# One transfer a unit for the sums of squared keys, and an earlier place for the end of feed-forward, in a fused two-layer block

## The chip, the cores and the metric

The kernel is one program on one core of a Trainium2 chip. The metric is the device time of one execution in microseconds, from the median of several runs. A core has TensorE for matrix products (PE in the profile; PEld is its weight load), VectorE (DVE), ScalarE (ACT), GpSimd (POOL) and SyncE (SP), which here only issues DMA transfers. Every engine works through its own list of instructions in order and waits on semaphores. 16 DMA engines carry the transfers of all of them.

## The reference

Batch 4, 512 positions, width 512, context 512 x 256, all in float32. Two layers stand one behind the other, each with a mixing step and a feed-forward step:

```
x = x + tanh(g_xattn[0]) * mamba(ctx, z=layernorm(x))        # 512 channels, 16 states, a scan over 512 positions
x = x + tanh(g_ffn[0])   * bit_ffn(layernorm(x))             # gate/val/out, 512 x 2048, ternary weights, 8-bit rows
x = x + tanh(g_xattn[1]) * attn(layernorm(x), ctx)           # 16 heads of 128, rmsnorm on q and k
x = x + tanh(g_ffn[1])   * experts(layernorm(x))             # 4 experts, row i goes to expert i % 4

# in attn:
k = (ctx @ Wk).reshape(B, S, 16, 128);  v = (ctx @ Wv).reshape(B, S, 16, 128)
k = k * rsqrt(mean(k ** 2, axis=-1) + 1e-5) * gk
```

The keys and values depend on the context alone. For each of 4 batches and 16 heads the kernel computes the keys, and for each key the mean of squares and its power -1/2.

## The kernel before

Six streams of work are written out as lists: Q (the ternary weights are made from the float weights), M (the scan, `MAMBA`, per batch b), F (the first feed-forward, `FFN`, per batch), K (keys and values, `KV`), A (attention, `ATTN`, 64 heads j = 16 b + head) and E (the experts). Each stream has a generator for every engine that yields once per item. `plan()` merges the streams: it gives each item the engines and times that are written in `mamba`, `forward`, `keys` and so on (microseconds, estimates in the source), their needs and PSUM banks, and always takes the item that can start first, ties by `FIRST`. What comes out is one fixed order of streams for each engine. At run time nothing is reordered: an instruction that waits holds up all that stand behind it on its engine.

**Keys and values, K.** A unit is (b, q): batch b and heads 4q to 4q+3; n = 4q + b runs from 0 to 15. In a unit TensorE forms four key blocks (`k`, L780) and four value blocks (`v`, L785), and ScalarE copies them to `ks` (three buffers; L1379, L1385) and squares the keys (L1382). Then `n` (L791) sums the squares by a product with ones, into four rows of a bank; `nv` (ScalarE, L1390) writes mean plus eps of these to `ksr`, of which there is one, after it has waited for the transfers out of `ksr` of the unit before. `r` (SP, L1742) issues four transfers from rows 0, 32, 64 and 96 of `ksr` to 32 partitions x 16 columns of `krs` each. `pw` (GpSimd, L1503) raises 128 x 16 values to -1/2, and `st` (SP, L1746) stores them to `rk_scratch`. `pw` and `st` of a unit stand in the next unit. Keys and values go to memory from SP, L1718 and L1724; the weights of the next group of heads are fetched at L1631 and L1636, in the places `v` 0 and `v` 3 of the last batch's unit. Attention's queries use the region of `ksr`.

**The scan, M.** For each of 32 steps VectorE runs a product (L1020), a scan (L1025) and a product (L1032) on 128 x 1024, ScalarE forms the decay (L1290), and GpSimd issues a transfer that adds the term to `u` (L1534), from one of three buffers. For b = 0 the factors come from TensorE (L666, L670).

**The first feed-forward, F.** For each group t of 128 rows: entry `e` 0 (statistics), 1 (quantization, VectorE), 2 (transposes), `o` (GpSimd adds a bias to x); then `m`, even numbers TensorE and ScalarE, odd ones VectorE, for four chunks of 512 of the hidden width; then leaving, `l` 0 (quantization of h, L1065 and L1069), `l` 1 and 2 (transposes L736, copies L1359), `l` 3 (the output product, L746) and `l` 4 (the addition to x, L1147). The leaving of group t stands between the items of group t+1. When all four groups are through, the list `XT` follows: `st` (statistics, L924, and deviation on GpSimd) for four t, `hn` (normalization, L1159) for four t, `xt` (transposes L758, copies L1368) for four t. `hn` writes over h. Attention of a batch (`q`, L806) needs all four `xt`.

M of batch 0, Q and K run first, F of batch 0 behind M, then attention of batch b beside M and F of batch b+1, at the end the experts.

## Time and profile before

| | us |
|---|---|
| median of 3 runs | 1853.01 (1847.89 to 1858.5) |
| the profiled execution, its time | 1852.26 |
| its span, first to last instruction | 1850.5 |
| TensorE busy | 1763.2 (95%) |
| VectorE busy | 1300.1 (70%) |
| ScalarE busy | 963.8 (52%) |
| GpSimd busy | 666.5 (36%) |
| mean granted clock of TensorE | 0.983 |

The profile comes from one execution. Its page gives the busy time of each engine and 40 slices of the span; the trace behind it answers for stretches, lines of the source, waits (an engine's idle time just before an instruction, and what ended it), DMA issues with their time to landing, and the chain of work that ended last. The granted clock is the share of full speed that TensorE had. A row of the timeline may merge neighbours of one kind, with their count behind an x.

### The profile page before, as it was taken

Reading aid. Unit: us, or ns where it says so; the run is one execution under the profiler, and the core shown is the slowest. Engines: PE = TensorE matmul, PEld = TensorE weight load, DVE = VectorE, ACT = ScalarE, POOL = GpSimd, SP = SyncE. Lnnn points to the kernel's source line nnn. Section 1 sums busy time; section 2 is a strip of 40 time slices with the busy share of each in tenths; the row PEclk is TensorE's granted clock in tenths of the full one; section 3 lists DMA queues with packets and bytes.
Section 4 is the critical chain, followed back from the end, with each engine's and each line's share of the span. In section 5 each row is a group of like instructions: output and inputs, shape, how many; then the busy total and the mean of one; then the engine's idle time right before and its main releaser. Section 6 shows DMA issues by size and latency. Waiting matters only on the chain.

```text
span 1850.5 us, 19507 instructions
## 1 busy us (share of the span) xinstructions
PE 1763.2 (95%) x6114; PEld 809.9 (44%) x6114; DVE 1300.1 (70%) x1899; ACT 963.8 (52%) x1920; POOL 666.5 (36%) x696
## 2 busy tenths in 40 slices
PE   8999899879999999999999999999999899999999
PEld 4333344334444444444444444444444344445543
DVE  4989686989998689899787998987652444422221
ACT  7988786446545546566455566555435334320100
POOL 2434322337463324557222564562223333310000
PEclk9999899979999999999999999999999999999999
DMA  7999833767851146897212589732112799837110
GB/s 262 242 289 286 244 109 116 203 164 187 199 142 57 51 100 162 208 240 200 66 30 74 156 188 251 199 95 69 35 57 91 218 282 293 236 119 273 40 51 28
DMA packets 159045, 292.11 MB, mean 158 GB/s; under 512 B 18424, under 2 KB 51704, under 8 KB 156000
## 3 DMA queue, kind: packets, MB, share of 16 engines
q1 hardware_dynamic: 141664, 227.95, 39.0%
q0 software_dynamic: 17280, 62.92, 17.5%
q8 instruction: 50, 0.82, 0.2%
q14 instruction: 51, 0.42, 0.1%
HBM read 169.51 MB, written 58.26 MB: 123 GB/s over the span
## 4 chain that ended last, share of the span: by engine, by line
PE 72%; DVE 13%; ACT 6%; issue 4%; DMA 3%; POOL 1%; SPq 1%; DVEq 0%; ACTq 0%; POOLq 0%
PE p L846 11%; PE p L806 10%; PE p L823 9%; PE p L857 8%; PE p L893 6%; PE p L697 5%; DVE s_M L1025 5%; PE p L780 4%; PE p L829 4%; PE p L908 3%; PE p L746 3%; PE p L785 3%; DVE s_M L1020 2%; DVE s_M L1032 1%; DVE s_U L1178 1%
## 5 line engine op out<-in xcount | busy, mean ns | idle before, releaser
L1025 DVE TENSOR_TENSOR_SCAN s_M<-s_M 128x1024 f32<-128x1024 f32 x128 | 296.4, 2315 | 9.9 <-ACT s_M L1290 7.6
L1178 DVE CUSTOM_DVE_ANT_0 s_U<-p,s_U 128x512 f32<-128x512 f32 x256 | 188.2, 745 | 161.0 <-PE p L823 159.7
L823 PE MATMUL p<-s_U 128*128 128x512 f32 x512 | 268.2, 612 | 4.6 <-DVE s_U L1178 3.0
L806 PE MATMUL p<-s_U 128*128 128x512 f32 x512 | 256.7, 610 | 3.4 <-ACT s_U L1418 2.7
L1534 POOL DMA_DIRECT2D s_u<-s_M x120 | 111.7, 931 | 383.7 <-DVE s_M L1032 355.6
L1579 POOL TENSOR_SCALAR s_U<-s_U 128x512 f32<-128x512 f32 x256 | 231.9, 926 | 6.3
L857 PE MATMUL p<-s_U 128*128 128x512 f32 x512 | 223.7, 593 | 0.0
L846 PE MATMUL p<-s_U 128*128 128x512 f32 x472 | 216.0, 599 | 2.5 <-ACT s_U L1431 2.4
L1431 ACT COPY s_U<-p 128x512 f32<-128x512 f32 x196 | 105.5, 594 | 176.3 <-PE p L829 175.0
L1290 ACT ACTIVATE s_M<-s_dl,s_small 128x511 f32<-128x511 f32 x256 | 170.3, 717 | 35.5 <-DVE s_M L1025 35.3
L1426 ACT ACTIVATE s_U<-s_U 128x512 f32<-128x512 f32 x256 | 181.6, 710 | 5.3
L1575 POOL TENSOR_TENSOR s_U<-s_U,s_mone 128x4 f32<-128x4 f32 x64 | 81.7, 1277 | 201.1 <-ACT s_U L1426 201.0
L857 PEld LDWEIGHTS p<-s_U 128*128 128x128 f32 x512 | 96.8, 190 | 119.0 <-issue 118.1
L806 PEld LDWEIGHTS p<-s_U 128*128 128x128 f32 x512 | 96.1, 197 | 106.3 <-issue 87.1
L846 PEld LDWEIGHTS p<-s_U 128*128 128x128 f32 x472 | 89.9, 192 | 113.8 <-issue 108.0
L780 PE MATMUL p<-s_U 128*128 128x512 f32 x256 | 120.2, 615 | 18.9 <-ACT s_U L1390 10.8
L1503 POOL TENSOR_TENSOR s_U<-s_U,s_mhalf 128x4 f32<-128x4 f32 x64 | 80.7, 1261 | 136.7 <-ACT s_U L1418 136.0
L823 PEld LDWEIGHTS p<-s_U 128*128 128x128 f32 x512 | 88.2, 193 | 83.1 <-issue 77.8
L697 PE MATMUL p<-s_wq,s_U 128*128 128x512 fp8e4 x512 | 121.6, 380 | 0.0
L785 PE MATMUL p<-s_U 128*128 128x512 f32 x256 | 119.6, 601 | 2.1 <-ACT s_U L1382 1.5
L1032 DVE TENSOR_TENSOR s_M<-s_M,s_bc 128x1024 f32<-128x1024 f32 x96 | 119.8, 1248 | 1.4
L1020 DVE TENSOR_TENSOR s_M<-s_du,s_bc 128x1024 f32<-128x1024 f32 x96 | 116.8, 1216 | 0.0
(194 smaller groups left out, 2458.3 us busy)
## 6 DMA issues: line engine op xcount, KB each, us to landing
s_u<-s_M POOLq DMA_DIRECT2D x120, 512.0 KB, 7.6
s_bc<-bc_scratch SPq DMA_DIRECT2D x96, 256.0 KB, 4.5
k_scratch<-s_U SPq DMA_DIRECT2D x16, 1024.0 KB, 7.9
v_scratch<-s_U SPq DMA_DIRECT2D x16, 1024.0 KB, 5.4
s_U<-in_Wq SPq DMA_DIRECT2D x64, 256.0 KB, 6.6
s_U<-k_scratch SPq DMA_DIRECT2D x64, 256.0 KB, 5.4
s_U<-rk_scratch SPq DMA_DIRECT2D x64, 256.0 KB, 5.8
s_U<-in_Wo SPq DMA_DIRECT2D x64, 256.0 KB, 4.5
```

Of the source, the lines that this page charges most:

```text
L697: ins = e.matmul(banks[bk][:], xT[t % 2][:, k, :], wt[:, k, ch * 512:(ch + 1) * 512], start=False, stop=(k == 3))
L780: ins = e.matmul(banks[bk][:], wk[:, k, i * 128:(i + 1) * 128], cT[b][:, k, :], start=(k == 0), stop=(k == 1))
L785: ins = e.matmul(banks[bk][:], cT[b][:, k, i * 128:(i + 1) * 128], wv[:, k, :], start=(k == 0), stop=(k == 1))
L806: ins = e.matmul(banks[bk][:], wqq[j % 2][:, k, :], axT[b % 2][:, k, :], start=(k == 0), stop=(k == 3))
L823: e.matmul(banks[bk][:], qT[j % 3][:, k * 128:(k + 1) * 128], kT[j % 2], start=True, stop=True).then_inc(S["a_s"], 1)
L846: ins = e.matmul(banks[bk][:], V[v][:, kt, :], now[:, kt], start=(kt == 0), stop=(kt == 3))
L857: ins = e.matmul(banks[bk][:], OT[h][:, k * 128:(k + 1) * 128], wo[h], start=(i == 0), stop=(i == GH - 1))
L1025: e.tensor_tensor_scan(w, dA[i % 2], w, 0.0, ALU.mult, ALU.add).then_inc(S["m_s"], 1)
L1178: e.tensor_tensor_reduce(out=Pm[j % 2][:, k, :], in0=banks[ABANK[kind, j, k]][:], in1=rkb[j % 2], scale=rq[:, k:k + 1], scalar=-3.0e38, op ...
L1290: e.activation(av[:, t, 1:512], dl[:, 2 * g + t, 1:512], ACT.Exp, scale=Aneg[:, 2 * g + t, n:n + 1]).then_inc(S["m_da"], 1)
L1426: e.activation(Pm[j % 2][:, k, :], Pm[j % 2][:, k, :], ACT.Exp, bias=nm[:, k:k + 1], scale=1.0, accum_out=sm[:, k:k + 1]).then_inc(S["a_e" ...
L1579: e.tensor_scalar(P, P, rc[:, k - 1:k], 1.0, ALU.mult, ALU.mult).then_inc(S["a_pd"], 1)
```

## The change

- `ksr` becomes two buffers, used in turn; `nv` waits for the transfer two units before (unit 1 for the first product that read the region).
- `r` becomes one transfer, from the four rows of `ksr` to a new array `rs_scratch` in memory, 2 KB a row. It stands before `v` 3.
- A new item `ld` loads the 16 rows of four units, as 128 partitions x 64 columns of `krs`; it waits for the four transfers. `pw` comes four times, on 16 columns each, and `st` once, 128 x 64, both per four units. They stand in the units of the next group of heads: `ld` behind `k` 1 of its first unit, `pw` behind `k` 3, `st` in the second unit.
- `rk_scratch` has another order of rows; the loads of its rows in attention follow. Attention's first rows wait for the first store only, and before heads 4, 8 and 12 SP waits for the store of their group.
- The store of the keys and the fetch of the next `wk` move to the place of `k` 3.
- In `ffn_order` both transposes `l` 1 and 2 of the group before stand behind `m` 2, `l` 3 behind `m` 4, `l` 4 behind `m` 5; the next entry's statistics come before `m` 3, its `o` and transposes behind `m` 6.
- `XT` goes. `st` of groups 0 to 2 stands behind `l` 0 of group 3, `hn` and `xt` of these behind `l` 3, and `st`, `hn`, `xt` of group 3 last. `st` waits for the addition of its own group.
- Two semaphores are merged into others (`d_dtw` into `d_ipw`, `f_pad` into `p_set`); the planner's times follow.

```diff
-            order += [("m", t, 2 * c)] + (leave[:1] if c == 0 else []) + [("m", t, 2 * c + 1)] + (leave[3:] if c == 2 else leave[c + 1:c + 2] if c < 2 else [])
-            if c:
-                order += enter[:1]
-                enter = enter[1:]
-        order += enter
+            order += [("m", t, 2 * c)] + (leave[:1], leave[1:3], leave[3:4], enter[2:])[c]
+            order += (enter[:1] if c == 1 else []) + [("m", t, 2 * c + 1)] + (leave[4:] + enter[1:2] if c == 2 else [])
         leave = [("l", t, k) for k in range(5)]
-    return order + leave
+    order += leave[:1] + [("st", t, 0) for t in range(3)] + leave[1:4] + [("hn", t, 0) for t in range(3)] + [("xt", t, 0) for t in range(3)]
+    return order + leave[4:] + [("st", 3, 0), ("hn", 3, 0), ("xt", 3, 0)]
...
-XT = [("st", t) for t in range(4)] + [("hn", t) for t in range(4)] + [("xt", t) for t in range(4)]
...
 for q in range(4):
     for b in range(NB):
-        last = ((b - 1) % NB, q - (b == 0))
-        KV += [(b, q, "k", i) for i in range(4)] + [(b, q, "v", 0), (b, q, "v", 1), (b, q, "n", 0), (b, q, "v", 2), (b, q, "nv", 0)]
-        KV += [(*last, "pw", 0)] if q or b else []
-        KV += [(b, q, "v", 3), (b, q, "r", 0)] + ([(*last, "st", 0)] if q or b else [])
-KV += [(NB - 1, 3, "pw", 0), (NB - 1, 3, "st", 0)]
+        first, second = q > 0 and b == 0, q > 0 and b == 1
+        KV += [(b, q, "k", 0), (b, q, "k", 1)] + ([(NB - 1, q - 1, "ld", 0)] if first else []) + [(b, q, "k", 2), (b, q, "k", 3)]
+        KV += [(NB - 1, q - 1, "pw", i) for i in range(4)] if first else []
+        KV += [(b, q, "v", 0), (b, q, "v", 1), (b, q, "n", 0)] + ([(NB - 1, q - 1, "st", 0)] if second else [])
+        KV += [(b, q, "v", 2), (b, q, "nv", 0), (b, q, "r", 0), (b, q, "v", 3)]
+KV += [(NB - 1, 3, "ld", 0)] + [(NB - 1, 3, "pw", i) for i in range(4)] + [(NB - 1, 3, "st", 0)]
...
-        ksr = U[:, 26624:27136]
+        ksr = [U[:, o:o + 512] for o in (26624, 25600)]
...
-                        if n:
-                            e.wait_ge(S["d_ksr"], 64 * n)
-                        e.activation(ksr, banks[bk][:], ACT.Copy, bias=EPS, scale=1.0 / HD).then_inc(S["k_nv"], 1)
+                        if n == 1:
+                            e.wait_ge(S["m_xp"], 1)
+                        elif n:
+                            e.wait_ge(S[f"d_ksr{n % 2}"], 16 * (n // 2))
+                        e.activation(ksr[n % 2], banks[bk][:], ACT.Copy, bias=EPS, scale=1.0 / HD).then_inc(S["k_nv"], 1)
...
-                        n = NB * q + b
-                        power(krs[:, 16 * n:16 * n + 16], (S["d_ksr"], 64 * (n + 1)), "k_p")
+                        power(krs[:, 64 * q + 16 * i:64 * q + 16 * i + 16], (S["d_kr"], 16 * (q + 1)), "k_p")
...
-                    if kind == "v" and i == 0:
+                    if kind == "k" and i == 3:
                         if b == NB - 1 and q < 3:
                             load_kw(q + 1)
-                    elif kind == "v" and i == 1:
                         e.wait_ge(S["k_kc"], 4 * n + 4)
...
                         e.wait_ge(S["k_nv"], n + 1)
-                        for h in range(4):
-                            e.dma_start(krs[32 * h:32 * h + 32, 16 * n:16 * n + 16],
-                                        ksr[32 * h:32 * h + 1, :].rearrange("o (p c) -> o p c", c=16)).then_inc(S["d_ksr"], 16)
+                        e.dma_start(rsd[16 * q + 4 * b:16 * q + 4 * b + 4], ksr[n % 2][0:128:32, :]).then_inc(S[f"d_ksr{n % 2}"], 16)
+                    elif kind == "ld":
+                        e.wait_ge(S["d_ksr0"], 32 * (q + 1))
+                        e.wait_ge(S["d_ksr1"], 32 * (q + 1))
+                        e.dma_start(krs[:, 64 * q:64 * q + 64], rsd[16 * q:16 * q + 16].rearrange("r (p c) -> (r p) c", c=64)).then_inc(S["d_kr"], 16)
                     elif kind == "st":
-                        e.wait_ge(S["k_p"], n + 1)
-                        e.dma_start(rkd[j:j + 4].rearrange("h (p c) -> (h p) c", c=16), krs[:, 16 * n:16 * n + 16]).then_inc(S["d_rk"], 16)
+                        e.wait_ge(S["k_p"], 4 * (q + 1))
+                        e.dma_start(rkd[16 * q:16 * q + 16].rearrange("r (p c) -> (r p) c", c=64), krs[:, 64 * q:64 * q + 64]).then_inc(S["d_rk"], 16)
```

## Rows read from the trace of the kernel before

**Rows 1.** The page: busy time of TensorE; DMA share in 40 slices, tenths.

```profile
PE 1763.2 (95%) x6114; PEld 809.9 (44%) x6114; DVE 1300.1 (70%) x1899; ACT 963.8 (52%) x1920; POOL 666.5 (36%) x696
...
DMA  7999833767851146897212589732112799837110
```

**Rows 2.** Windows of 20 us: length, then busy times, clock, DMA share, GB/s; sums.

```profile
360.00:380.00 20.00, 9.51 (x40) 4.40 (x38) 19.52 (x24) 7.11 (x12) 6.63 (x7) 0.83 0.92 231
...
sum 840.00, PE 785.04 PEld 351.45 DVE 712.25 ACT 541.88 POOL 338.69; mean PE 18.69 PEld 8.37 DVE 16.96 ACT 12.90 POOL 8.06
...
sum 1020.00, PE 978.15 PEld 458.48 DVE 587.83 ACT 421.93 POOL 327.85; mean PE 19.18 PEld 8.99 DVE 11.53 ACT 8.27 POOL 6.43
```

**Rows 3.** Windows of 5 us around the large stall, same columns.

```profile
195.00:200.00 5.00, 0.00 (x0) 0.00 (x0) 0.00 (x0) 0.00 (x0) 0.00 (x0) 0.64 1.05 300
200.00:205.00 5.00, 4.10 (x5) 1.85 (x6) 3.18 (x4) 3.47 (x6) 3.03 (x2) 0.50 0.70 265
```

**Rows 4.** The chain that ended last: start, us, what.

```profile
186.89 13.29 DMA s_krs<-s_U
...
200.90 6.55 PE p L780 x8
207.89 3.43 PE p L780 x8
```

**Rows 5.** Timeline, 181 to 201 us: start, duration, instruction, idle before it.

```profile
181.40 0.36 SPq L1724 DMA_DIRECT2D v_scratch<-s_U  x1
...
200.24 2.90 POOL L1503 TENSOR_TENSOR s_krs<-s_krs,s_mhalf 128x16 f32<-128x16 f32 x1 [8.14 <-DMA s_krs<-s_U]
...
200.90 3.78 PE L780 MATMUL p<-s_U 128*128 128x512 f32 x4 [6.63 <-ACT s_U L1390]
```

**Rows 6.** DMA issues of 180 to 202 us: median us to landing last.

```profile
v_scratch<-s_U SPq DMA_DIRECT2D x1, 1024.0 KB, 18.1
```

**Rows 7.** Timelines of TensorE and of SP around the fetches of keys’ weights.

```profile
77.00 3.60 PE L780 MATMUL p<-s_U 128*128 128x512 f32 x8
...
94.45 6.02 PE L780 MATMUL p<-s_U 128*128 128x512 f32 x10 [5.36 <-DMA s_U<-in_Wk]
...
162.88 3.67 PE L780 MATMUL p<-s_U 128*128 128x512 f32 x8 [2.49 <-DMA s_U<-in_Wk]
...
82.59 1.14 SPq L1631 DMA_DIRECT2D s_U<-in_Wk  x1
```

**Rows 8.** Timeline of VectorE, around 105 us.

```profile
105.35 1.22 DVE L1020 TENSOR_TENSOR s_M<-s_du,p 128x1024 f32<-128x1024 f32 x1 [5.57 <-PE p L666]
```

**Rows 9.** The tile krs: its instructions, min/median/max ns.

```profile
L1742 SPq DMA_DIRECT2D s_krs<-s_U x64: 513/1036/1937, 41.8 to 366.6; - x64
L1503 POOL TENSOR_TENSOR s_krs<-s_krs,s_mhalf x16: 2903/4174/5304, 54.1 to 368.7; 128x16 f32<-128x16 f32 x16
```

**Rows 10.** Timeline, 376 to 386 us.

```profile
376.93 0.72 DVE L1147 SCALAR_TENSOR_TENSOR s_x<-p,s_fq,s_x 128x512 f32<-128x512 f32 x1
377.69 0.69 DVE L924 BATCH_NORM_STATS2 s_U<-s_x 128x6 f32<-128x512 f32 x1
...
380.81 0.64 POOL L1512 TENSOR_TENSOR s_U<-s_U,s_mhalf 128x1 f32<-128x1 f32 x1
...
381.57 3.65 PE L758 MATMUL p<-s_identf,s_U 128*128 128x128 f32 x16 [5.52 <-DVE s_U L1159]
...
385.93 6.19 PE L806 MATMUL p<-s_U 128*128 128x512 f32 x8 [0.72 <-issue]
```

**Rows 11.** Timeline of GpSimd, 85 to 91 us.

```profile
85.51 5.30 POOL L1503 TENSOR_TENSOR s_krs<-s_krs,s_mhalf 128x16 f32<-128x16 f32 x1
90.66 1.04 POOL L1534 DMA_DIRECT2D s_u<-s_M  x1
```

**Rows 12.** DMA issues, 60 to 200 us, and one of the whole run.

```profile
s_krs<-s_U SPq DMA_DIRECT2D x32, 2.0 KB, 7.3
...
bc_scratch<-s_M SPq DMA_DIRECT2D x3, 64.0 KB, 1.6
```

91 lines of the change are left out of this document (38 added, 53 removed).

## The prediction

> **What bounds the kernel now.** I read four views in this order: the page's busy times, the table of 20 us windows, the timeline of TensorE with its idle gaps, and for each large gap the chain and the waits of the other engines. TensorE is busy 1763.2 us of a span of 1850.5 us [rows 1]; the two halves of the window table give the same sum, 785.04 up to 840 us and 978.15 behind [rows 2]. Only idle TensorE time, 87.3 us in all, and time at its lower clock can be won by a new order. Of the idle time 55 us (840 less 785.04) lie before 840 us. There the kernel has two weak places. Up to about 210 us the DMA engines are full [rows 1], and TensorE waits for things that land late. Near 370 us the keys and values are used up, attention can't start, and TensorE is busy 9.51 of 20 us [rows 2]. After 420 us attention fills nearly every gap, so I expect what is won before to be carried to the end, and nothing to be won there.
>
> **The one large stall, around 195 us.** In 195 to 200 us no engine has any busy time, while the DMA share is 1.05 [rows 3]. ScalarE's `nv` (L1390) of unit 9 wants to overwrite the only `ksr`, whose four transfers of unit 8 are still on their way: the last was issued at 186.89 and landed 13.29 us later [rows 4]. GpSimd, which waits for the same transfers, ran at 200.24, and TensorE at 200.90 after 6.63 us idle, behind ScalarE's L1390 [rows 5]. The clock had fallen to 0.50 in 200 to 205 us [rows 3], the 1.2 GHz level, after 5 us without any matmul; eight matmuls took 6.55 us where the next eight took 3.43 [rows 4], so 3.1 us more were lost. Together 9.7 us. The change has two `ksr`, and `nv` waits for the transfer of two units before, so this wait goes. What is late next is a buffer of three, `ks`: the values of unit 8 were issued at 181.40 [rows 5] and took 18.1 us [rows 6], so they landed at 199.5, and the first key copy of unit 10 goes into their buffer. TensorE finished unit 9 at about 194.3 (200.90 less 6.63). It has three banks for k0 to k2, three times 1.72 us (half of 3.43 us), so it works to 199.5; k3 waits for ScalarE's two passes after 199.5, some 1.2 us. I take 9.7 less 1.2 = **8.5 us saved**, with ends 3 and 9.7: the low end holds if the DMA backlog itself makes all three wait until 199.5 or later (6.63 us idle less the 5.2 us from 194.3 to 199.5 leaves 1.4 us, and about half of the 3.1 us of clock, 3 in all).
>
> **The weights of the second group of heads.** TensorE waited 5.36 us, to 94.45, for `in_Wk` [rows 7], and VectorE in turn 5.57 us for a broadcast that stood behind those products [rows 8]. The weights may be fetched when the 16th key product is done, at 80.6 (77.00 plus 3.60), but the queue of SP was then in four `krs` transfers, a store and another load, and issued at 82.59 [rows 7]. The change replaces four issues of 1.036 us (median, up to 1.937) by one [rows 9], drops 12 of 16 stores, and puts the fetch two places earlier. That gives 82.59 less 80.7 = **1.9 us**. Ends: 0, since the 11.7 us of landing are the DMA engines' and not SP's, and 5.4 if the load also overtakes the 1 MB load ahead of it. The third group's fetch had 2.49 us of idle too, but was issued as the product ended; I give it nothing. Over 16 units the change takes 48 issues and 12 stores off SP, some 50 us times one microsecond; nearly all is hidden, as SP mostly waits for engines.
>
> **The end of the first feed-forward.** Before, the statistics of all four row groups wait for the last one. VectorE's last addition to x is at 376.93 (0.72 us, to 377.65), and the first product of attention starts at 385.93 [rows 10]: 8.3 us. Here run four statistics, GpSimd's two small steps, four normalizations, 16 transposes and a copy. After, three groups are through while the output product of the last group runs, and one remains. Three statistics of 0.8 us (the first at 377.69, 0.69 us and the aggregation behind it) leave the path, 2.4 us, and three quarters of the 3.65 us of transposes, 2.7 us. GpSimd's steps on the one group, hidden behind the next group's statistics before, now stand in the open: 0.64 us for the power and, as an estimate, as much again for the small step and the handovers, 1.3 us [rows 10]. 2.4 + 2.7 less 1.3 = **3.8 us saved**. VectorE does three statistics and three normalizations, some 4 us, in front of the last addition instead of behind it; they stand where it ran steps of the next scan while TensorE formed the output product, so they push those and not the addition. Without this cover they would cost their 4 us, and the saving would be 0. Ends 0 and 6: the latter if the shorter gap also spares the lower clock some two of the microseconds that it took from what follows 380 us, as it took 3.1 us behind the other gap.
>
> **The reordered middle of feed-forward.** TensorE now forms the second chunk's products before the first transposes, and both transposes stand together; VectorE's entry statistics come one product earlier. Per row group the same instructions run. Three of the four feed-forwards run beside attention, where other products are at hand: behind 840 us all causes together leave some 32 us idle (87.3 less 55) in a thousand. I take 0, with ends minus 2 and plus 3 us, a tenth of that. The joined semaphore of the first two weights costs nothing: they are issued one behind the other, and TensorE waits for the first at most once, while it still warms up.
>
> **What is added.** The squared sums go out to memory, come back as 64 columns for four units together, are raised to the power in four pieces, and go out again. The power work is the same, 16 pieces of 4.17 us median [rows 9], none of it on the end's path; but four stand in a row now, three times. GpSimd also issues the accumulating transfers of the scan (L1534), about every 5 us. A piece of 5.30 us beside a busy VectorE (2.90 when all was idle, [rows 5]) just fits between two of them: from 85.51, with the next issue at 90.66 [rows 11]. Four in a row are late by some 0.6 to 1 us each, 2.4 to 4 us per group, of which the landing slack takes a part. And there are two new waits in order: SP waits before the load for the last unit's store, and GpSimd before the first piece for the load. Behind SP's wait stand the next key store and weight loads; behind GpSimd's stand the accumulating transfers, and behind these VectorE's scan, which needs their buffers. The cover is two products on either side and the values between, about 8 us. An 8 KB transfer in the full stretch lands in 7.3 us (median of 32) and on a quiet queue a store of 64 KB in 1.6 us [rows 12]. At 7.3 us for each, store, load and issues take some 16 us against 8 to 12 us of cover; that is paid at most at the two group ends in the full stretch, less what the scan's three buffers absorb. I take **plus 3 us** for all of this, nearest to the single pieces that were absorbed; ends 0 and 12.
>
> The Trainium skill ("DMA: Bandwidth & Descriptors", the anatomy of one DMA) puts a fixed 2.0 us on each transfer, most of it the write receipt of the target memory. By that figure the store and the load would be an estimated 4 us, under the cover, and the sum would end 3 us lower, at 1838. The trace agrees for the quiet queue (1.6 us) and not for the full one (7.3 us), so the rows decide.
>
> **The sum.** 8.5 + 1.9 + 3.8 less 3 = 11.2 us. The profiled execution took 1852.26 us, 1.76 us more than its span, and lies 0.75 us below the median of the three runs, inside their spread. 1852.26 less 11.2 is **1841 us**.
>
> **The rivals.**
> (1) *The DMA engines bound the first 200 us.* For it: the share stays at about 1 from 60 to 200 us [rows 1], and the age of the backlog was 18.1 us [rows 6]. Then one wait gives way to the next: 3 us from the large stall, 0 from the weights, 3.8 from the tail, and 1 us of new waits remain against: 5.8 us, 1846.5. Against it: the share fell to 0.70 right behind the stall [rows 3], so the backlog ended there.
> (2) *GpSimd's order becomes the bound, the kernel is slower.* At the group ends near 97 and 168 us the store and the load each land as late as the slowest seen, 13.3 us [rows 4]; with issues 28.6 us against 10 us of cover. Each end then stops GpSimd, the scan and, through ScalarE's decays, TensorE for 18 us; twice 18 less 14.2 gives plus 22, 1874. It decides from 12 us per end (two of them beyond 14.2 plus 9.3). Against it: no such transfer but that one took so long, and scan and products have their own slack.
> (3) *More is won than counted.* The stall goes entirely, the weights overtake the load, the tail spares the clock, no new wait: 9.7 + 5.4 + 6 = 21, 1831.
> (4) *The large stall doesn't go*, since `nv` of unit 9 finds another wait of the same length (the `ks` buffer and the accumulating transfers land as late): 1.9 + 3.8 less 3, about 1849.5.
>
> **How the numbers follow.** Chances: forecast 0.43, (1) 0.20, (3) 0.18, (4) 0.12, (2) 0.07. About 0.5%, or 9.3 us, is what a measurement of this kernel can tell from no change: the bounds are 1843.7 and 1862.3. The forecast's own range, 1834 to 1849, lies two thirds to three quarters below 1843.7; with (3) and a little of (1) this gives 0.54 for faster. Slower is (2) with its larger half, 0.06; the rest, 0.40, is no change. The range from 1829 to 1852 leaves out (2) and the edges.
>
> **What would show it.** The 195 to 200 us window has busy engines and TensorE no gap above 2 us for L1390; SP issues `in_Wk` within 0.3 us of the 16th key product; from the last addition to x to the first product of attention it is about 4.5 us; GpSimd shows waits for the loaded squares of 0 to 6 us near 97 and 168 us, and four powers in a row; behind 420 us TensorE's idle time stays within 3 us of before. The prediction is wrong if the powers or their wait stop VectorE's scan for more than 6 us in all, or if the ScalarE wait at 193 us returns under another name.

## The result, and the profile after

The changed kernel takes 1859.43 us (median of 20 runs, 1851.65 to 1862.68), the kernel before 1851.78 us in the same comparison (20 runs, 1845.78 to 1858.5): a ratio of 1.0037, interval 1.0025 to 1.0049. The forecast was 1841 us with a range of 1829 to 1852, so the time moved the other way and lies outside the range. The profiled execution of the changed kernel took 1859.95 us, its span is 1858.2 us.

The page of the changed kernel: busy time, TensorE's clock and the DMA share, as in [rows 1].

```profile
PE 1767.5 (95%) x6114; PEld 808.6 (44%) x6114; DVE 1303.7 (70%) x1899; ACT 965.5 (52%) x1919; POOL 676.3 (36%) x696
...
PEclk9999999989999999999999999999999999999999
DMA  7999833688761138878113579822122799847110
```

TensorE is busy 4.3 us more for the same 6114 products, GpSimd 9.8 us more. The large stall is gone. Below are the same windows of 5 us as in [rows 3], and the last addition of feed-forward and attention's first product, as in [rows 10].

```profile
195.00:200.00 5.00, 5.00 (x13) 1.98 (x11) 3.38 (x2) 4.36 (x8) 4.83 (x4) 1.00 0.98 288
200.00:205.00 5.00, 5.00 (x18) 1.97 (x18) 3.63 (x6) 3.77 (x7) 4.83 (x5) 1.00 1.05 306
```

```profile
365.06 0.75 DVE L1139 SCALAR_TENSOR_TENSOR s_x<-p,s_fq,s_x 128x512 f32<-128x512 f32 x1 [1.65 <-PE p L742]
...
372.66 1.53 PE L798 MATMUL p<-s_U 128*128 128x512 f32 x3 [0.72 <-issue]
```

The first product of attention starts at 372.66 instead of 385.93, 13.3 us earlier. So the gains came, and were lost later. Behind 420 us TensorE is idle 45.4 us of 1430.5 before and 55.7 us of 1438.2 after (length, then TensorE's busy time, before and after):

```profile
420.00:1850.50 1430.50, 1385.14 (x4935) 650.09 (x4933) 958.97 (x1509) 664.06 (x1457) 524.54 (x580) 0.99 0.52 142
...
420.00:1858.20 1438.20, 1382.48 (x4895) 646.28 (x4894) 962.67 (x1508) 661.03 (x1443) 530.35 (x577) 0.99 0.52 141
```

The next table tells where, for this and all kernels below. Each row is one profiled execution, while executions of one kernel differ by some 10 us, so a difference of two or three us in one cell is not yet a property of the kernel. Its marks are starts of instructions in the timeline: q0 is the sum of squares of the first query (ScalarE, L1394 here), w*k* is VectorE's first addition of the output of head group *k* (L1177 here, four heads a group, sixteen groups), "end" the last addition of the experts. All in us; the last column is the measured ratio to before.

| kernel | scan step 32 | q0 | q0 to w0 | w0 to w3 | w3 to w7 | w7 to w11 | w11 to end | ratio |
|---|---|---|---|---|---|---|---|---|
| before | 228.5 | 392.7 | 85.1 | 287.0 | 344.6 | 322.6 | 414.9 | 1 |
| changed kernel | 222.9 | 378.0 | 91.1 | 290.7 | 352.3 | 324.0 | 418.6 | 1.0037 |
| two_ksr | 218.1 | 382.2 | 83.0 | 285.4 | 344.7 | 322.6 | 419.6 | 0.9958 |
| tks_one | 218.1 | 382.8 | 83.0 | 285.3 | 347.5 | 322.6 | 415.9 | 0.9975 |
| tks_kw | 217.5 | 381.9 | 82.9 | 285.3 | 347.5 | 322.6 | 419.7 | 0.9971 |
| pin_spread | 218.9 | 389.7 | 83.0 | 285.3 | 344.6 | 322.6 | 419.5 | 1.0007 |
| pin_grp | 233.8 | 409.4 | 82.9 | 285.3 | 344.6 | 322.6 | 415.7 | 1.0104 |
| k_only | 220.3 | 397.3 | 85.2 | 287.9 | 347.6 | 322.6 | 418.9 | 1.0074 |
| f_only | 229.6 | 390.5 | 87.1 | 286.6 | 345.7 | 326.3 | 415.5 | 1.0018 |
| tks_fmid | 219.8 | 382.2 | 84.5 | 291.2 | 347.4 | 323.5 | 421.8 | 0.9997 |
| tks_ftail | 221.2 | 385.6 | 83.0 | 285.5 | 352.2 | 324.8 | 418.3 | 1.0029 |
| tks_f | 221.9 | 382.8 | 87.2 | 286.5 | 345.6 | 326.3 | 418.1 | 0.9999 |
| pw4 | 225.6 | 387.1 | 83.3 | 285.4 | 347.6 | 322.6 | 418.5 | 0.9986 |
| tks_pw4 | 226.0 | 389.6 | 83.7 | 287.0 | 344.6 | 322.6 | 416.5 | 0.9996 |
| after_pw3 | 219.8 | 376.0 | 93.6 | 287.0 | 351.3 | 324.1 | 419.2 | 1.0046 |
| after_ld12 | 229.6 | 385.3 | 83.6 | 286.6 | 345.2 | 324.7 | 417.1 | 1.0012 |
| pin_late | 221.3 | 378.3 | 100.9 | 290.4 | 348.4 | 324.1 | 421.8 | 1.0089 |
| late_pw | 223.6 | 378.3 | 111.3 | 283.2 | 349.1 | 326.3 | 418.7 | 1.0146 |

Against before the changed kernel stands at -14.7 us at q0, then loses 6.0, 3.7, 7.7, 1.4 and 3.7: +7.8 at the end. In these five stretches TensorE's idle time grows by 4.8, 2.8, 0.6, 2.0 and 4.8 us (the last up to the end of the span); the rest is busy time.

**The 6.0 us behind q0.** In the timeline of the changed kernel, 377 to 402 us:

```profile
377.32 0.32 SPq L1721 DMA_DIRECT2D s_krs<-rs_scratch  x1
...
384.48 3.47 POOL L1489 TENSOR_TENSOR s_krs<-s_krs,s_mhalf 128x16 f32<-128x16 f32 x1 [11.00 <-DMA s_krs<-rs_scratch]
...
387.92 0.91 POOL L1520 DMA_DIRECT2D s_u<-s_M  x1
388.56 1.35 POOL L1489 TENSOR_TENSOR s_U<-s_U,s_mhalf 128x4 f32<-128x4 f32 x1
...
389.94 0.75 DVE L1166 CUSTOM_DVE_ANT_0 s_U<-p,s_U 128x512 f32<-128x512 f32 x1 [4.71 <-POOL s_U L1489]
...
398.19 6.01 POOL L1489 TENSOR_TENSOR s_krs<-s_krs,s_mhalf 128x16 f32<-128x16 f32 x1
...
401.74 0.66 PE L805 MATMUL p<-s_U,s_ones 128*32 128x128 f32 x8 [6.43 <-ACT s_U L1394]
```

SP issues the last group's load at 377.32, GpSimd has waited for it since 373.5 and runs the first power at 384.48. Behind it stand the scan's accumulation and the power of attention's first query, for which VectorE's first score waits 4.71 us. Two more powers of the keys follow, and the last stands behind the power of the second head's query. TensorE's wait of 6.43 us is for ScalarE, which had waited 7.50 us for the late scores. A second new wait is smaller: the first query's copy on ScalarE now waits for the last transfer out of `ksr` (before, the third head's did), to 377.37, where its product had ended at 376.33. In the full stretch the same load is no better: the first row is the landing of the two loads of 60 to 200 us (size, median us), the second GpSimd's wait at the second group end, in the timeline. The third shows a wait of TensorE that no term had: the third group's `in_Wv` was issued at 166.55, behind the new transfer of the squares, and landed 12.6 us later. In two_ksr below it was issued at 161.39 and TensorE waited 0.88 us. Why it landed so late stays open.

```profile
s_krs<-rs_scratch SPq DMA_DIRECT2D x2, 32.0 KB, 13.5
```

```profile
184.44 4.78 POOL L1489 TENSOR_TENSOR s_krs<-s_krs,s_mhalf 128x16 f32<-128x16 f32 x1 [7.93 <-DMA s_krs<-rs_scratch]
```

```profile
179.19 3.50 PE L777 MATMUL p<-s_U 128*128 128x512 f32 x4 [6.03 <-DMA s_U<-in_Wv]
```

**The 7.7 us between w3 and w7.** Whole windows from w3 to w7, before and changed: length, TensorE busy (count), its weight load, VectorE, ScalarE, GpSimd, clock, DMA share, GB/s. Then the two windows of 20 us of the changed kernel with a lower clock; before they are at 1.00. The last row looks inside one of them: 0.53 over 7 us, so for most of it TensorE had its lower level, 1.2 GHz.

```profile
764.80:1109.50 344.70, 334.73 (x1285) 157.42 (x1284) 297.93 (x433) 201.58 (x423) 157.32 (x158) 1.00 0.55 141
...
960.00:980.00 20.00, 19.44 (x78) 7.43 (x77) 7.13 (x11) 10.14 (x20) 3.71 (x5) 1.00 0.19 56
1060.00:1080.00 20.00, 16.68 (x66) 8.58 (x67) 19.86 (x24) 11.40 (x26) 13.91 (x10) 1.00 0.81 196
```

```profile
759.80:1112.10 352.30, 341.70 (x1285) 159.51 (x1284) 309.52 (x439) 201.99 (x424) 160.38 (x160) 0.98 0.56 142
...
960.00:980.00 20.00, 19.09 (x75) 6.91 (x74) 13.91 (x34) 10.28 (x14) 2.29 (x2) 0.83 0.11 36
1060.00:1080.00 20.00, 16.66 (x45) 7.41 (x46) 18.06 (x18) 10.44 (x24) 13.10 (x10) 0.83 0.87 209
...
967.00:974.00 7.00, 6.87 (x23) 2.08 (x24) 6.38 (x13) 5.17 (x7) 0.00 (x0) 0.53 0.00 0
```

The 1285 products are the same, and the idle time too (10.0 and 10.6 us). But TensorE is busy 7.0 us longer: in two windows the granted clock fell to 0.83, and 0.17 of 20 us is 3.4 us each. No instruction of the change stands here but reordered items of the feed-forward. Just ahead of the second fall TensorE had been idle 2.22 us, to 1062.08, in the changed kernel; at the same place before it was idle 1.74 us, to 1061.71, and the clock stayed.

This explains the stretch in these two executions and not the result. Over its 20 executions the changed kernel's mean granted clock is 0.9842; in the runs below, the kernel before has 0.9831 to 0.9846. As an estimate, one less the clock, times the span, is the most that the lower clock can cost: 29 us in the changed kernel, 28 to 31 before. The two profiled executions give 33 and 31. So the lower clock can't account for the 7 to 8 us of the result. The idle time can: behind 420 us it is 10.4 us more.

### The profile page after: what moved, and what is told of

The parts are those of the page before. It is cut to its first block, busy times and chain, and to the rows that moved or that the text cites. A ratio compares the mean times of both kernels' runs of the same rounds, so it can differ in the third digit from the quotient of the medians.

```text
span 1858.2 us, 19459 instructions
## 1 busy us (share of the span) xinstructions
PE 1767.5 (95%) x6114; PEld 808.6 (44%) x6114; DVE 1303.7 (70%) x1899; ACT 965.5 (52%) x1919; POOL 676.3 (36%) x696
## 4 chain that ended last, share of the span: by engine, by line
PE 67%; DVE 14%; issue 6%; POOL 5%; ACT 4%; DMA 4%; SPq 0%; DVEq 0%; ACTq 0%; POOLq 0%
PE p L838 10%; PE p L815 8%; PE p L798 8%; PE p L849 7%; PE p L885 6%; PE p L693 6%; DVE s_M L1017 5%; PE p L772 3%; PE p L821 3%; PE p L900 3%; PE p L777 3%; PE p L742 3%; DVE s_M L1012 2%; DMA s_u<-s_M 2%; DVE s_M L1024 2%
## 5 line engine op out<-in xcount | busy, mean ns | idle before, releaser
L1017 DVE TENSOR_TENSOR_SCAN s_M<-s_M 128x1024 f32<-128x1024 f32 x128 | 297.1, 2321 | 10.5 <-ACT s_M L1278 7.9
L1520 POOL DMA_DIRECT2D s_u<-s_M x120 | 117.1, 975 | 350.7 <-DVE s_M L1024 322.1
L1560 POOL TENSOR_SCALAR s_U<-s_U 128x512 f32<-128x512 f32 x256 | 237.9, 950 | 6.4
L1556 POOL TENSOR_TENSOR s_U<-s_U,s_mone 128x4 f32<-128x4 f32 x64 | 82.1, 1283 | 223.6 <-ACT s_U L1412 223.6
L798 PEld LDWEIGHTS p<-s_U 128*128 128x128 f32 x512 | 94.9, 194 | 106.3 <-issue 91.1
L772 PE MATMUL p<-s_U 128*128 128x512 f32 x256 | 121.1, 620 | 13.3 <-ACT s_U L1376 8.6
L821 PE MATMUL p<-s_identf,s_U 128*128 128x128 f32 x784 | 106.0, 277 | 19.2 <-DVE s_U L1166 9.1
```

What stands on the lines that cost most here:

```text
L772: ins = e.matmul(banks[bk][:], wk[:, k, i * 128:(i + 1) * 128], cT[b][:, k, :], start=(k == 0), stop=(k == 1))
L798: ins = e.matmul(banks[bk][:], wqq[j % 2][:, k, :], axT[b % 2][:, k, :], start=(k == 0), stop=(k == 3))
L1017: e.tensor_tensor_scan(w, dA[i % 2], w, 0.0, ALU.mult, ALU.add).then_inc(S["m_s"], 1)
L1560: e.tensor_scalar(P, P, rc[:, k - 1:k], 1.0, ALU.mult, ALU.mult).then_inc(S["a_pd"], 1)
```

## Experiments

Theory A: what is won ahead of 400 us is carried to the end, and the loss is the new waits and powers of GpSimd. Theory B: the later stretches have a bound of their own and give any gain back. Theory C: the loss comes from the new order that the planner makes of everything, not from what the instructions cost. Every ratio is against executions of the kernel before that were taken beside the run, and is the better measure; the kernel before's own median moved by up to 2.9 us from one such set to another. Where the text gives us between two runs, they are medians unless it says otherwise.

### Parts of the change alone

**two_ksr.** Before, with only this, the waits that follow from it and the two merged semaphores:

```diff
-        ksr = U[:, 26624:27136]
+        ksr = [U[:, o:o + 512] for o in (26624, 25600)]
...
-                            e.wait_ge(S["d_ksr"], 64 * n)
-                        e.activation(ksr, banks[bk][:], ACT.Copy, bias=EPS, scale=1.0 / HD).then_inc(S["k_nv"], 1)
+                            e.wait_ge(S[f"d_ksr{n % 2}"], 64 * (n // 2))
+                        e.activation(ksr[n % 2], banks[bk][:], ACT.Copy, bias=EPS, scale=1.0 / HD).then_inc(S["k_nv"], 1)
```

> The kernel before with two buffers for the mean squares, and nothing else moved: four transfers a unit as before, the same order on every engine. It takes away the wait at 193 us and leaves all orders alone. Theory A (what is won in the first 400 us is carried to the end; the changed kernel loses it again by its new waits on GpSimd): 5 to 9 us faster than before, about 1845. Theory B (later stretches have a bound of their own, VectorE's scans or the loads, so that an earlier start of attention is given back whatever the order): within 3 us of before. Theory C (the new order of all engines behind 400 us is what costs): as A, for the order here is the old one.

1842.48 us, ratio 0.9958 (0.9943 to 0.9973). 10.4 us ahead at step 32; in the table the middle columns repeat those of before to within 2.1 us, and nothing is given back up to w11. The last stretch takes 4.7 us more than before, but the two kernels with the same middle columns, tks_one and pin_grp, have 415.9 and 415.7 there, so this differs from one execution to the next. A said 5 to 9 us faster, it is 9.0. Theory B falls.

**k_only.** The key part without the feed-forward part.

> Only the part on the keys: one transfer a unit, load, four powers and store per four units; feed-forward's order as before. Theory A: the loss sits here; GpSimd waits about 11 us for the last load and then has four powers in front of attention's first steps; 5 to 10 us slower than before. Theory B: within 3 us of before. Theory C: anything within 10 us of before, with its loss spread over all stretches behind 400 us.

1864.77 us, ratio 1.0074 (1.0055 to 1.0092): 13 us slower than before, outside the 5 to 10 us of A and the 10 us of C. In its order the last group's powers stand ahead of the layer normalization:

```profile
375.93 2.94 POOL L1506 TENSOR_TENSOR s_krs<-s_krs,s_mhalf 128x16 f32<-128x16 f32 x1 [16.08 <-DMA s_krs<-rs_scratch]
...
386.67 0.19 POOL L1513 TENSOR_SCALAR s_U<-s_U 128x1 f32<-128x1 f32 x1
...
388.23 4.04 PE L759 MATMUL p<-s_identf,s_U 128*128 128x128 f32 x16 [11.90 <-DVE s_U L1160]
```

GpSimd waited 16.08 us for the load, the deviations came behind three powers, and TensorE's transposes waited 11.90 us. Its mean clock is 0.978 over five executions, the lowest here; by the estimate above that is up to 9 us more than before.

**f_only.** The feed-forward part without the key part.

> Only the part on feed-forward: the new order of its items and the early statistics, transposes and copies; keys as before. Theory A: 2 to 5 us faster than before (the shorter end of the first feed-forward, no new wait). Theory B: within 3 us. Theory C: a loss of 3 to 8 us, behind 440 us.

1855.99 us, ratio 1.0018 (1.0001 to 1.0035). q0 comes 2.2 us earlier than before, but q0 to w0 takes 2.0 us and w7 to w11 3.7 us more. The gain of 2 to 5 us that A expected did not come; 4.5 us more by the medians and 3.3 by the ratio fit C.

**tks_one.** two_ksr, with one transfer a unit to `rs_scratch` and one load a unit from it; powers as before.

```diff
-                        for h in range(4):
-                            e.dma_start(krs[32 * h:32 * h + 32, 16 * n:16 * n + 16],
...
+                        e.dma_start(rsd[4 * n:4 * n + 4], ksr[n % 2][0:128:32, :]).then_inc(S[f"d_ksr{n % 2}"], 16)
...
+                    if m >= 0 and kind == "v" and i == 0 or kind == "pw" and n == 15:
+                        e.wait_ge(S[f"d_ksr{m % 2}"], 16 * (m // 2 + 1))
+                        e.dma_start(krs[:, 16 * m:16 * m + 16], rsd[4 * m:4 * m + 4].rearrange("r (p c) -> (r p) c", c=16)).then_inc(S["d_kr"], 16)
```

> Kernel before with two ksr buffers, and with one transfer a unit to rs_scratch and one load a unit from it (placed in the next unit's place v 0) in place of the four from row to 32 partitions; powers still unit by unit. Theory A (the transfers are no cost, the grouping of load and powers is): within 2 us of two buffers alone, 1841 to 1845 us. Rival D (the way over memory costs: two hops in a full queue make GpSimd wait for each unit): GpSimd waits for the load over 20 us in all and the time is above 1847 us. Rival E (fewer packets free the DMA engines in the first 200 us): below 1840 us.

1844.82 us, ratio 0.9975 (0.9963 to 0.9987). Step 32 is at 218.1 as in two_ksr, and the other columns agree up to w3; in w3 to w7 the clock was 0.83 in 1040 to 1060 us, where two_ksr had 1.00. By the medians it is 2.3 us slower than two_ksr, by the ratios 3: the way over memory is no gain and at most a small cost.

### The grouped powers on a held order

In the next two runs the planner lays out the kernel before, and the new entries of the keys' stream are set into its lists; all other entries of every engine keep their order.

**pin_grp.**

```diff
+        for b, q, kind, i in KV:
+            anchor = {"ld": (0, q + 1, "k", 1) if q < 3 else (NB - 1, 3, "pw", 0), "pw": (NB - 1, q, "pw", 0), "r": (b, q, "v", 3),
+                      "st": (1, q + 1, "n", 0) if q < 3 else (NB - 1, 3, "st", 0)}.get(kind, (b, q, kind, i))
```

> The key part of the change (one transfer a unit, load, four powers and store per four units) on top of the order of the kernel before: the planner lays out the kernel before, its list of every engine is kept, and only the entries of the keys' own stream are set into it, the powers of a group in the place of the power of its last unit, the last group's at the end of the keys. So the rest of each engine's list is that of the kernel before with two buffers (1842.5 us). Theory A (GpSimd's waits for the load and the grouped powers cost directly): 1850 us or more, with the loss at the three group ends and in front of attention's first head. Theory C (the loss of the key part comes from the order that the planner makes of the whole behind it): 1840.5 to 1845 us, with waits of GpSimd for the load that leave no mark on the milestones.

It moves the keys' store and the fetch of `wk` too, as the change does.

1867.66 us, ratio 1.0104 (1.0082 to 1.0126): 25 us above two_ksr. Its timeline at the first group end:

```profile
114.28 13.51 POOL L1540 TENSOR_TENSOR s_krs<-s_krs,s_mhalf 128x16 f32<-128x16 f32 x4 [3.54 <-DMA s_krs<-rs_scratch]
...
127.75 1.80 POOL L1571 DMA_DIRECT2D s_u<-s_M  x2
132.47 1.22 DVE L1055 TENSOR_TENSOR s_M<-s_du,p 128x1024 f32<-128x1024 f32 x1 [6.78 <-DMA s_u<-s_M]
```

Four powers take 13.51 us of GpSimd. Two accumulations leave late, at 127.75, and VectorE waits 6.78 us for the landing of one, since its three buffers are full. The scan, 1.0 us ahead of two_ksr at step 16, is 8.0 behind soon after this block (step 23), 15.7 by step 32, 20.6 when the second batch's scan starts, and 28.1 behind the last one near 382 us (27.2 at q0). From q0 to w11 every stretch has two_ksr's length to 0.1 us: a loss is carried as a gain is. Up to half of the loss can be the lower clock: its mean is 0.979 here and 0.985 in two_ksr, and the estimate from it 40 against 28 us.

**pin_spread.** The same, with the powers of groups 0 to 2 one in each unit of the next group.

```diff
-        KV += [(NB - 1, q - 1, "pw", i) for i in range(4)] if first else []
...
+        KV += [(NB - 1, q - 1, "pw", b)] if q else []
+        KV += [(b, q, "r", 0), (b, q, "v", 3)] + ([(NB - 1, q - 1, "st", 0)] if q and b == NB - 1 else [])
```

> As the run with the key part on the order of the kernel before (1867.7 us, 25 us above two buffers alone), with one edit: the four powers of groups 0 to 2 stand one in each unit of the next group, in the places where the kernel before has its powers, and the store behind the last of them; one transfer a unit and one load a group stay, and the last group keeps its four powers in a row. Theory A1 (blocks of four powers, 13.5 us of GpSimd each, hold up the scan's accumulation; transfers and load are no cost): the 20.6 us lost up to scan step 32 go, and the loss near 380 us stays, 1847 to 1852 us. Rival A2 (the load and the wait for it cost): at least 5 us of the 20.6 stay, 1855 us or more.

1850.81 us, ratio 1.0007 (0.9989 to 1.0024). Of the 20.6 us up to the second scan 0.9 are left: transfers and loads are nearly free, the block is what costs. The last group's block remains and costs 7.5 us at q0 against two_ksr:

```profile
363.35 12.58 POOL L1540 TENSOR_TENSOR s_krs<-s_krs,s_mhalf 128x16 f32<-128x16 f32 x4 [5.41 <-DMA s_krs<-rs_scratch]
```

```profile
PE p L793 <- DVE s_U L1194: 10.5, 1, 10.5
```

The second block is of its waits, 330 to 400 us (total, count, longest): the transposes of the normalized rows waited 10.5 us once. The whole difference to two_ksr is 8.3 us, as A1 expected.

### The last group's powers in the changed kernel

**late_pw.** The changed kernel, these powers planned behind the third head's exponentials. The loads of the output weights, which waited behind their store on SP, move to the place of the load.

```diff
-"pw": [("K", at.get((b, q, "ld", 0)))]
+"pw": [("K", at.get((b, q, "ld", 0)))] + ([(NB, "ex", 2, 3)] if q == 3 else [])
```

> The changed kernel, only the four powers and the store of the last group of heads are planned behind the exponentials of attention's third head; the transfer that loads their input stays where it is. Theory A (the loss is made by GpSimd's wait for that transfer and the four powers in front of attention's first head; what is won ahead of 400 us is carried to the end): no wait of about 11 us of GpSimd near 380 us, the first score on VectorE near 380 instead of 390 us, and the time falls by 5 to 10 us against the changed kernel, to 1850 to 1855 us. Theory B (what is won ahead of attention is given back later whatever it is): first score earlier, end within 3 us of the changed kernel, 1857 to 1862 us. Theory C (the planner's order behind 400 us decides): a time that follows neither, with the milestones between 450 and 800 us moving by more than the first score does.

**pin_late.** The changed kernel's own order, these entries moved on GpSimd and SP alone.

```diff
+        ks = [i for i, s in enumerate(l) if s == "K"][KV.index((NB - 1, 3, "pw", 0)):]
+        to = [i for i, s in enumerate(l) if s == "A"][ATTN.index(("rc", 2, 3))]
+        order[e] = [s for i, s in enumerate(l[:to + 1]) if i not in ks] + ["K"] * len(ks) + [s for i, s in enumerate(l) if i > to and i not in ks]
```

> The changed kernel with its own order held on every engine, but the last group's four powers and store moved on GpSimd and SyncE behind the last reciprocal of attention's third head. Nothing else moves. Theory A: the wait of 11 us and the powers in front of attention leave the path, first score near 380 us, the output product of the first heads 6 to 10 us earlier, and that lead is carried: 1849 to 1853 us. Theory B or C: the lead is gone by 700 us, and the time is within 3 us of the changed kernel, 1856 to 1862 us.

1875.98 us (1.0146, 1.0123 to 1.0168) and 1866.1 us (1.0089, 1.0063 to 1.0114): both slower than the changed kernel, where I expected 5 to 10 us less. late_pw loses 20 us between q0 and w0; the planner changed the rest there too, so what of it is the powers' I can't tell. In pin_late it can be read:

```profile
388.21 0.75 DVE L1171 CUSTOM_DVE_ANT_0 s_U<-p,s_U 128x512 f32<-128x512 f32 x1 [3.28 <-PE p L820]
...
432.92 12.34 POOL L1494 TENSOR_TENSOR s_krs<-s_krs,s_mhalf 128x16 f32<-128x16 f32 x4
445.24 0.69 POOL L1565 TENSOR_SCALAR s_U<-s_U 128x512 f32<-128x512 f32 x1
...
446.08 1.08 PE L826 MATMUL p<-s_identf,s_U 128*128 128x128 f32 x4 [11.59 <-POOL s_U L1565]
```

The first score comes at 388.21, only 1.7 us before the changed kernel's 389.94. With GpSimd free it waits for TensorE, whose list has the second head's query first and ran it at the lower clock (eight products in 6.56 us from 380.60; in the changed kernel 5.40 us). By the second head's first score the lead is 4.8 us (pin_late, then the changed kernel):

```profile
396.51 0.75 DVE L1171 CUSTOM_DVE_ANT_0 s_U<-p,s_U 128x512 f32<-128x512 f32 x1
...
401.35 0.75 DVE L1166 CUSTOM_DVE_ANT_0 s_U<-p,s_U 128x512 f32<-128x512 f32 x1 [2.86 <-POOL s_U L1489]
```

It still is 4.8 us at the third head's first score and 4.5 at the fourth's. Then the block stands in front of the division of a head's scores (L1565), TensorE waits 11.59 us for it, and at the fifth head's first score the lead has become 9.5 us of delay. So GpSimd's wait and its powers in front of attention cost the changed kernel some 4.8 us, most of its 6.0 behind q0, and the place I moved the block to cost 14.

### The feed-forward part on two buffers

two_ksr with the reordered middle (tks_fmid), with the new end of the list (tks_ftail), with both (tks_f). The diffs are those of the change.

> Kernel before with two ksr buffers and the new middle order of the first feed-forward alone (transposes, output product, addition and next statistics moved; the list behind the last group as before). The prediction put this edit at 0 (-2 to +3). With the end of the list alone the same kernel took 1853.9 us, with both 1848.8, with none 1842.5. If the middle order gains 5 us by itself: 1837 to 1840 us. If it only mends what the moved end does to the plan: 1841 to 1850 us.

> Kernel before with two ksr buffers, and of the feed-forward part all but the new middle order: the statistics and turned rows of groups 0 to 2 stand ahead of the last group's output. Keys and powers as before, unit by unit. Theory A: both early gains add (10 to 14 us for the buffers, about 1 to 4 for the tail) and are carried: 1838 to 1841 us, attention's first query 12 us or more ahead of before. Theory C (the feed-forward part sets another order of GpSimd and VectorE later, as the feed-forward part alone suggests with 0.2% more time): 1843 to 1847 us with the loss behind 450 us.

> Kernel before with two ksr buffers and the whole feed-forward part of the change; keys and powers as before, unit by unit. It differs from the changed kernel in the key part's transfers, loads and grouped powers alone. If the new middle order costs (theory M, for the feed-forward part alone came out 0.2% above before): 2 to 4 us more than the same kernel without the middle order. If it is free: the same within 2 us. Sum of the two parts run alone: 1842.5 + 3.3, 1846 us. Theory A for the whole: this kernel at least 10 us below the changed kernel, since its powers stand one by one.

1849.9 us (0.9997, 0.9975 to 1.0018), 1853.91 (1.0029, 1.0014 to 1.0044) and 1848.79 us (0.9999, 0.9985 to 1.0014), against 1842.48 (0.9958) with none: by the ratios 7, 13 and 8 us more. The two don't add. tks_fmid is at the slow end of what was expected, tks_ftail 7 us above even C's range, and tks_f, expected level with tks_ftail or 2 to 4 us above it, is 5 us below. tks_f is 10.6 us below the changed kernel, as A said. In tks_f step 32 comes 3.8 us later than in two_ksr, before any item of the feed-forward has run. As no instruction of that time differs, I put this down to the order, from one execution of each. Between this step and q0 it wins 3.2 us of them back. The rest is lost behind q0.

### The planner's order by itself

Each of these changes one number in the planner and no instruction: its time of a power or of the load.

```diff
-"pw": [("POOL", 3.0)]
+"pw": [("POOL", 4.0)]
```

> The kernel before, with the planned time of one power step 4.0 in place of 3.0 us, and nothing else: no instruction is changed, only the order that the planner makes of them. Theories A and B: within 3 us of before. Theory C (the planner's order of all later items swings with small changes of its times): 3 us or more away from before, to either side.

> Kernel before with two ksr buffers and the planner's time of a power at 4.0 us; the instructions are those of two buffers alone, the lists of VectorE, ScalarE, GpSimd and SyncE differ in places. If the order's part (2.6 us less in the kernel before) adds to the buffers': 1838 to 1841 us. If the order's part depends on where the stalls are: anywhere from 1841 to 1849 us.

pw4, on the kernel before: 1849.54 us, ratio 0.9986 (0.9974 to 0.9999), 2 to 2.6 us less and so under the 3 us that C asked for. tks_pw4, the same edit on two_ksr: 1849.33 us, 0.9996 (0.9979 to 1.0013), 7 us above two_ksr for the same instructions and at the slow edge of what was expected. This is the clearest sign that the order by itself can cost. Its products waited once 4.0 us for `in_Wv`, where two_ksr's waited 0.9.

**after_pw3.** The reverse edit on the changed kernel.

> The changed kernel; only the planner's time of a power is 3.0 us as in the kernel before, in place of 4.0. The instructions are the same, the order of VectorE, GpSimd and SyncE differs in places. Theory A: within 2 us of the changed kernel (1857 to 1861 us), for the load and the powers stay where they are. Theory C (the planner's order sets the end): a shift of 3 us or more, with no counterpart in what is removed or added.

1858.79 us, ratio 1.0046 (1.0029 to 1.0063): within 2 us of the changed kernel, against C.

**after_ld12.** The changed kernel with `"ld": [("DMA", 12.0)]` for 3.0.

> The changed kernel; only the planner's time for the load of a group is 12 us in place of 3 (9.1 to 17.9 us is what the transfer took in its trace), so the powers are planned later and the order of the rest shifts. Theory A: GpSimd's waits for the load shrink and the time falls 3 to 8 us against the changed kernel. Theory C: the time moves by 3 us or more in either direction, and the milestones behind 450 us change by more than the waits for the load do.

1851.78 us, ratio 1.0012 (0.9996 to 1.0027): 0.25% or 5 us less than the changed kernel by the ratios, 8 by the medians. GpSimd's waits for the load shrink from 18.9 us in two to one:

```profile
381.14 3.87 POOL L1489 TENSOR_TENSOR s_krs<-s_krs,s_mhalf 128x16 f32<-128x16 f32 x1 [1.12 <-DMA s_krs<-rs_scratch]
```

```profile
755.60:1100.80 345.20, 335.39 (x1285) 157.50 (x1284) 310.96 (x441) 205.00 (x428) 158.26 (x161) 1.00 0.58 148
```

It is 7.3 us later at q0 and level at w0: q0 to w0 takes 83.6 instead of 91.1. This supports A behind q0. From there w0 to w3 takes 286.6 instead of 290.7 and w3 to w7 (the window above) 345.2 instead of 352.3, with the clock back at 1.00. But this profiled execution is the fastest of its twelve (1847.95 us), and the mean clock over the executions is the same in both kernels (0.9845 and 0.9842). So the 7 us of that stretch are not shown to belong to the kernel, and C for w0 to w7 stays open.

### One term of the prediction by itself

**tks_kw.** two_ksr, with the store of the keys and the fetch of `wk` at the place of `k` 3.

```diff
-                    if kind == "v" and i == 0:
+                    if kind == "k" and i == 3:
                         if b == NB - 1 and q < 3:
                             load_kw(q + 1)
-                    elif kind == "v" and i == 1:
```

> Kernel before with two ksr buffers, and the store of the keys and the fetch of the next wk at the place of k 3 as in the change. By the prediction's term for in_Wk: 1.9 us less than two buffers alone, 1840 to 1841 us, if TensorE's wait at the group ends shortens and the transfers land no later. Rival: the DMA engines are full there, the landing moves with the issue, and the time is within 1 us of two buffers alone or above it.

1845.28 us, ratio 0.9971 (0.9954 to 0.9987): no gain over two_ksr, as the rival had it. The issue moved from 84.55 in two_ksr to 82.84 (timeline of SP), and TensorE's wait stayed (its waits of 90 to 100 us; two_ksr has the same 4.7):

```profile
82.84 0.77 SPq L1632 DMA_DIRECT2D s_U<-in_Wk  x1
```

```profile
PE p L779 <- DMA s_U<-in_Wk: 4.7, 1, 4.7
```

In the profiled execution it is as fast as two_ksr up to w3 and loses 2.8 us by w7, where the clock dropped in one window.

## Why the prediction was wrong

Two steps failed. "What is added" took four powers in a row as late by 2.4 to 4 us per group and left out the last group: a row holds GpSimd for 11.6 to 13.9 us, all of them cost 25 us on a held order, and the last group's stand in front of attention. And local gains were added up as gains of the whole kernel, "nothing to be won there" being read as nothing to be lost: behind 420 us TensorE's idle time grew by 10.4 us, where the prediction said within 3.

**The carrying of a gain** (what bounds the kernel). Right on a held order: two_ksr, pin_spread and pin_grp have the same lengths from w0 to w11 to a few tenths, while they differ by 27 us at q0. Wrong for the change, whose planned order is new in every stretch. w0 to w11 took 12.8 us more, 7.0 of them by the lower clock of this execution. Of the rows of before, 32 us of idle time in a thousand, I had read that attention fills its gaps; that this rests on one particular order they could not show, but the diff could: it changes costs and items that the planner reads. How much of the loss is the order and how much the new waits, no run separates.

**The large stall, 8.5 us (3 to 9.7).** The mechanism was right, the size slightly small. two_ksr alone is 10.4 us ahead at step 32, which holds this wait, the clock behind it and little else, and [rows 3] answer with a fully busy TensorE. That is above the high end of 9.7; on the whole kernel it is 9.0 us by the medians and 7.8 by the ratio.

**The weights of the second group, 1.9 us (0 to 5.4).** Wrong on the step "the issue moves by 1.9 us": in the changed kernel SP issued at 82.83, 0.24 us later than [rows 7]. And where it did come 1.7 us earlier, in tks_kw, TensorE's wait did not shrink: the low end. The row fits the reason given for it, a landing set by the full DMA engines.

**The end of the feed-forward, 3.8 us (0 to 6).** By itself it gave nothing. Between the addition of the scan's output to x (VectorE, 241.9 in the changed kernel) and q0, two_ksr takes 148.1 us, with this end 148.3, with the new middle 146.2, with both 144.8. Only the changed kernel gains much more there, 136.1 against 148.2 before. Before, TensorE waited 5.6 us for quantized rows and 5.5 for normalized ones (5.52 in [rows 10]); in the changed kernel both are under 0.4 us. With the end alone the two waits stay (5.6 and 6.0), and in tks_f one of 11.8 us takes their place. So some 3 us come with both edits and a further 8.8 only with the keys' part too. TensorE had more products at hand there (524 in this stretch, 512 in tks_f).

The step itself, by its own measure, gave less than 3.8 in the changed kernel: from the end of the last addition (365.81) to attention's first product it is 6.9 us, where 8.3 was before and about 4.5 was forecast, because the planner set a scan product of 1.22 us in front of the last statistics and GpSimd's small step took 2.07 us. The prediction had not seen that TensorE's own idle time is what counts there, and that key products were left for the gap:

```profile
366.26 1.07 PE L783 MATMUL p<-s_U,s_ones 128*32 128x512 f32 x8
...
367.26 3.70 PE L777 MATMUL p<-s_U 128*128 128x512 f32 x8
...
371.31 0.63 PE L750 MATMUL p<-s_identf,s_U 128*128 128x128 f32 x4 [0.35 <-DVE s_U L1147]
```

On the whole kernel both edits together cost some 8 us on two_ksr, which no term had.

**The middle, 0 (-2 to +3).** Not separable: 7 us more with the middle alone on two buffers, 5 us less when it is put on top of the end. Since edits of one planner number moved the time by 2 and 7 us, I don't call this a cost of the instructions.

**What is added, 3 us (0 to 12).** Two of its parts failed: "paid at most at the two group ends in the full stretch, less what the scan's three buffers absorb", and four in a row late by 2.4 to 4 us per group. A block takes 11.6 to 13.9 us (four blocks of pin_grp), since no accumulation lies between the pieces; the scan issues one about every 5 us and has three buffers, so the first block alone took the scan from 1.0 us ahead of two_ksr to 8.0 behind. On a held order all blocks together cost 25 us, 17 of them at groups 0 to 2, 8 at the last. In the changed kernel the planner set accumulations between the pieces, as a row at 189.18 shows. From 60 to 240 us VectorE waited there 4.9 us for landings of `u`, in five waits; before, it was 1.8 us in one:

```profile
189.18 0.90 POOL L1520 DMA_DIRECT2D s_u<-s_M  x1
189.81 4.90 POOL L1489 TENSOR_TENSOR s_krs<-s_krs,s_mhalf 128x16 f32<-128x16 f32 x1
194.68 0.91 POOL L1520 DMA_DIRECT2D s_u<-s_M  x1
```

Still, with tks_f at 0.9999 and the changed kernel at 1.0037, the key part's form and the order that comes with it cost 7 us against powers unit by unit, inside the range of 0 to 12; with the old feed-forward, two_ksr against k_only, it is 21 us. The last group stood in no term at all: there is no next group to hide it in, and it meets the layer normalization or attention's first head.

**The price of a transfer.** The loads of a group took a median of 13.5 us in the full stretch, nearly twice the 7.3 us that the prediction used; that row is of 2 KB transfers, a load is 32 KB. The Trainium skill ("DMA: Bandwidth & Descriptors", the anatomy of one DMA) has a fixed 2.0 us for a transfer, on the path of those that GpSimd issues; these loads are SP's. By it the term would have been smaller still, and the trace disagrees with it where the DMA engines are full.

**The rivals.** (2), the kernel slower by GpSimd's order, is in part the mechanism that came; it had 7 in 100 and 1874 us. It was set at the wrong place, the group ends near 97 and 168 us, and its condition of 12 us per end was not met (waits of 0 and 7.93 us). The largest wait, 11.0 us, was at 384 us. (1), (3) and (4) did not come: the stall went. In sum: 14.7 us ahead at q0, where 14.2 less 3 was forecast, then 22.5 us lost where nothing was.

**Split of the result**, by the ratios. One way: two buffers -0.42%, the feed-forward part on top +0.41%, the grouping on top of both +0.38%. The other way: two buffers -0.42%, the grouping on top +1.16% (k_only), the feed-forward part on top of both -0.37%. Both end at +0.37%. So the feed-forward part costs 8 us without the grouping and wins 7 with it, and neither has a price of its own. How much of each is order and how much instructions stays open, but for the 17 and 8 us on a held order. The fastest kernel of all is two_ksr.

## What to carry to other kernels

Before an item is batched, look at the engine that runs it: what else does that engine issue, how often is it needed, and how many buffers stand between? On a held order twelve short pieces in twelve gaps were nearly free, the same in three rows of four cost 17 us. Follow a batch to its last instance too, where no next unit covers it: the fourth row cost 8. And where a planner makes the order, a change of the items or of one cost is a new order everywhere: compare first on the old order with the new entries set in by hand, and only then with the planner free. Don't add up what two edits cost alone.

## What the runs showed of the hardware

- Two stretches of the same 1285 products and nearly the same idle time differed by 7 us through the granted clock. A window of 20 us at 0.83 in place of 1.00 costs 3.4 us, and the w3 to w7 column shows it: 344.6 and 344.7 without such a window (before, two_ksr), 347.5 with one in tks_one, 352.3 with two in the changed kernel. In 1060 to 1080 us both kernels idled 3.3 us, and only one lost the clock.
- The clock falls in one execution and not in another though the lists are the same: in 25 to 50 us it was 0.86 in pin_grp and 1.00 in pin_spread, whose lists differ only from the first group's powers on, behind 110 us. Over the executions of the kernel before the mean clock went from 0.978 to 0.989, mostly higher in the faster ones (0.989 at 1842.12 us, 0.980 at 1858.14 us).
- On GpSimd 128 x 16 powers took 2.89 to 2.94 us at best and up to 5.41 us in the first 200 us, beside the scan. What sets this is not shown: the piece at 122.0 in pin_grp took 2.89 us while VectorE ran its scan. Attention's 128 x 4 powers took 1.01 to 4.15 us, the longest where neighbouring records overlap.
